# Two of eight dense chunks moved inside the last attention group of a transformer block, with the weight split spread over earlier groups

## The reference, cut to what matters

```
x = x + layernorm(attention(layernorm(x)))          # 4 x 1024 tokens, width 128
x = x + layernorm(ffn(layernorm(x)))

attention: 16 heads of width 8, q and k with rotary embedding and gelu, causal softmax, out projection
ffn(xf):   out = swiglu(xf, sWg, sWu, sWd)          # shared expert, 128 -> 256 -> 128
           for e in range(8):                       # top 2 of 8 experts by a softmax router
               out += w[:, e] * swiglu(xf, Wg[e], Wu[e], Wd[e])
swiglu(x, wg, wu, wd) = (silu(x @ wg) * (x @ wu)) @ wd
```

## Time and profile before

| | |
|---|---|
| median of three runs | 803.59 us (802.44 to 805.21) |
| the profiled execution: its time, its span | 806.09 us, 804.4 us |
| mean granted TensorE clock | 0.952 |
| busy in the span: PE, DVE, ACT, POOL | 667.4, 610.2, 505.1, 323.1 us |
| attention group 15 | 560.8 to 592.6 us |
| its end to the first tile pair | 592.6 to 622.2 us |
| tile pairs 0 to 35 with chunks 4 and 5 | 622.2 to about 768 us |

### The profile page before, as it was taken

How to read it: one execution, slowest core, us unless ns; L and a number is a source line. 1 busy time by engine, 2 the same in 40 slices (tenths; PEclk the granted TensorE clock), 3 DMA queues, 4 the chain that set the end, 5 groups by cost and what they waited for, 6 DMA issues and landing times.

```text
span 804.4 us, 17228 instructions
## 1 busy us (share of the span) xinstructions
PE 667.4 (83%) x6081; PEld 323.6 (40%) x6112; DVE 610.2 (76%) x1262; ACT 505.1 (63%) x1055; POOL 323.1 (40%) x437
## 2 busy tenths in 40 slices
PE   5786368999989889899879899888888889799961
PEld 2332022333334324234324334323246777587741
DVE  5989758888887897987897987987526476455667
ACT  3655036787767878687778677778656544344653
POOL 3675111122212233172533163533453137776642
PEclk9999569999999999999999999999799999899995
DMA  6446451120131131240230321202603112363534
GB/s 155 137 152 171 120 164 21 50 50 21 33 76 31 22 76 47 57 107 15 61 76 29 75 70 47 65 29 63 202 27 107 40 51 81 83 191 98 158 105 129
DMA packets 88785, 66.18 MB, mean 82 GB/s; under 512 B 27728, under 2 KB 75249, under 8 KB 88703
## 3 DMA queue, kind: packets, MB, share of 16 engines
q1 hardware_dynamic: 80076, 54.24, 26.5%
q0 software_dynamic: 4352, 8.99, 3.4%
q10 hardware_dynamic: 4274, 1.87, 0.9%
HBM read 38.11 MB, written 24.46 MB: 78 GB/s over the span
## 4 chain that ended last, share of the span: by engine, by line
PE 45%; DVE 22%; ACT 7%; issue 6%; POOL 3%; DMA 3%; SPq 2%; POOLq 0%; ACTq 0%; DVEq 0%
DVE block_max L343 13%; PE ps L1998 11%; PE ps L2025 8%; PE ps L328 5%; PE ps L2105 3%; ACT expT L1453 3%; PE ps L335 3%; PE ps L1975 2%; SPq L1194 2%; PE ps L2086 2%; PE ps L2094 1%; PE ps L2063 1%; DMA q_space<-negT 1%; PE ps L2088 1%; PE ps L2087 1%
## 5 line engine op out<-in xcount | busy, mean ns | idle before, releaser
L1453 ACT ACTIVATE expT<-ps 128x512 f32<-128x512 f32 (+1 forms) x640 | 325.3, 556 | 134.8 <-PE ps L2025 129.7
L343 DVE TENSOR_REDUCE block_max<-ps 128x8 f32<-128x1024 f32 x288 | 340.0, 1218 | 57.6 <-PE ps L328 38.7
L1998 PE MATMUL ps<-expT,vr 128*9 128x256 f32 (+1 forms) x2560 | 181.8, 366 | 16.5 <-ACT x_in L1413 14.9
L2025 PE MATMUL ps<-q_space,k_space 64*128 64x512 bf16 (+3 forms) x768 | 165.8, 338 | 10.0 <-DMA q_space<-negT 6.6
L1370 POOL TENSOR_SCALAR_AFFINE_SELECT expT<-expT 128x512 f32<-128x512 f32 x128 | 83.0, 661 | 195.5 <-ACT expT L1453 195.4
L328 PE MATMUL ps<-k_space,q_space 64*128 64x128 bf16 (+3 forms) x1152 | 132.0, 280 | 34.7 <-DVE block_max L343 24.4
L2025 PEld LDWEIGHTS ps<-q_space,k_space 64*128 64x128 bf16 x768 | 46.0, 94 | 153.2 <-ACT expT L1453 102.4
L1385 POOL DMA_INDIRECT expert_rows<-expT,tile_to x72 | 70.0, 973 | 59.1 <-ACT expT L1488 40.4
L1998 PEld LDWEIGHTS ps<-expT,vr 128*9 128x9 f32 x2560 | 42.1, 89 | 98.9 <-issue 47.1
L328 PEld LDWEIGHTS ps<-k_space,q_space 64*128 64x128 bf16 x1152 | 49.5, 95 | 74.0 <-DVE block_max L343 58.3
L1323 POOL TENSOR_SCALAR negs<-block_max 128x32 bf16<-128x32 f32 x16 | 4.7, 296 | 133.1 <-DVE block_max L1575 133.1
(11 more groups left out here) (235 smaller groups left out, 927.4 us busy)
## 6 DMA issues: line engine op xcount, KB each, us to landing
expT<-sorted_rows SPq DMA_DIRECT2D x72, 65.0 KB, 1.9
expT<-expert_rows SPq DMA_DIRECT2D x14, 256.0 KB, 5.1
q_parts<-parts SPq DMA_DIRECT2D x24, 128.0 KB, 2.3
k_parts<-parts SPq DMA_DIRECT2D x24, 128.0 KB, 2.3
q_space<-q_parts SPq DMA_DIRECT2D x32, 96.0 KB
k_space<-k_parts SPq DMA_DIRECT2D x32, 96.0 KB
v_ones<-v_st SPq DMA_DIRECT2D x8, 288.0 KB, 3.0
vr<-v_ones SPq DMA_DIRECT2D x16, 144.0 KB
```

Of the source, the lines that this page charges most:

```text
L343: nc.vector.reduce_max(bm[:, g % 2, 2 * f:2 * f + 2, at:at + 4], ps[:, 2 * odd:2 * odd + 2].rearrange("p h (n k) -> p h n k", k=P), AX_X). ...
L1453: act.activation(expT[:, (NS * g + s) % PTN, hh, 0:width], ps[:, B_S + n % S_RING, 0:width], ACT.Exp, scale=SCALE).then_inc(exp_ok, 1)
L1998: last = nc.tensor.matmul(ps[32 * hh:32 * hh + VW, B_O, at:at + n], vr[:, g % RING, kt, hh * VW:(hh + 1) * VW], expT[:, (NS * g + s) % PTN ...
L2025: last = nc.tensor.matmul(ps[:, B_S + n % S_RING, col:col + m], head_rows(kr, g, hh, slice(kt * P, (kt + 1) * P)), head_rows(qr, g, hh, sl ...
```

## The change

The shared expert on chunks 0 and 1 is computed inside group 15, on all engines:

- TensorE gets six new entries in its list (`AHEAD`): the gate passes of a half stand at its slot and the up passes at the slot behind, and the 16 down matmuls of a chunk take two slots. The list of units after the group starts at unit 4 (`FIRST_U`), and `chain` is shifted with it.
- silu is computed as x * (1 + tanh(x / 2)) / 2: ScalarE takes the tanh, VectorE multiplies in two instructions, and keeps the down result (ScalarE did that).
- `rows_ahead` on VectorE makes high and low parts of these two chunks at the end of group 14. SyncE fetches the chunks' rows in group 14.
- `w_hi` is made by ScalarE and `w_lo` by GpSimd, one expert at a time (128x512), in groups 1, 2, 3, 8 and 12. The down weights are loaded in group 13, and the padding of the spare region in group 1, where before all this stood in SyncE's queue during group 15.
- The last pair's scatters start behind tile pair 7, five at a time (before: behind 4, three at a time). Pads are written behind the load of pair 15 (before 12). The bank for one projection changes, and a wait moves from the first row transposes to the first transposes of h.

```diff
+AHEAD_C = 2
+FIRST_U = 2 * AHEAD_C
+AHEAD = {5: ("half", 0, 0), 8: ("half", 0, 1), 18: ("down", 0, 0), 20: ("half", 1, 0), 26: ("half", 1, 1), 33: ("down", 1, 0)}
+SPLIT = {1: (0, 1), 2: (2, 3), 3: (4, 5), 8: (6, 7), 12: (8,)}
...
+            if g == G - 1 and slot in AHEAD:
+                order.append((g, slot, *AHEAD[slot], None))
...
-            B_ROWS, B_PROJ = (B_Y, B_HT), (B_ONE, B_XT)
+            B_ROWS, B_PROJ = (B_Y, B_HT), (B_ONE, B_HT)
...
+                    if (g, slot) == (1, 24):
+                        sp.wait_ge(empty_ok, 2)
+                        sp.dma_start(xs_d[SPARE:].rearrange("(n p) w -> p n w", p=P),
+                                     empty[:].unsqueeze(1).to_broadcast([P, NE, XW])).then_inc(padded, DMA)
+                    if g == G - 3 and slot in (8, 26):
+                        rows = slice(P * (slot > 8), P * (slot > 8) + P)
+                        sp.wait_ge(lo_ok, NE + 1)
+                        sp.dma_start(w_gu[:, 0:NE, rows], wd_d[:, rows, :].rearrange("e k h -> k e h")).then_inc(down_in, DMA)
...
+                    if g == G - 2 and slot in (12, 16, 20, 24):
+                        sp.wait_ge(pv_done, NS * (G - 2))
+                        get_turned((slot - 12) // 4)
...
-                PADS_AT, HALF = 13, LATE_T // 2
+                PADS_AT, HALF = 16, LATE_T // 2
...
+                def low_weights(e):
+                    pool.wait_ge(hi_ok, e + 1)
+                    nc.gpsimd.tensor_tensor(w_lo[:, e], w_gu[:, e], w_hi[:, e], ALU.subtract).then_inc(lo_ok, 1)
...
+                    for at, e in zip((4, 6), SPLIT.get(g, ())):
+                        if s == at:
+                            low_weights(e)
...
-                first, each_time = 4, 3
+                first, each_time = 7, 5
...
+                def high_weights(e):
+                    if e == 0:
+                        act.wait_ge(late_in, DMA * LATE)
+                    act.activation(w_hi[:, e], w_gu[:, e], ACT.Copy).then_inc(hi_ok, 1)
+
+                def tanh(p, c, i):
+                    act.wait_ge(sh_gate, 2 * c + i + 1)
+                    wait(act, sh_hu, 2 * (c - 1) + i + 1)
+                    act.activation(tanhs[:, i], ps[:, bank_of(p)], ACT.Tanh, scale=0.5).then_inc(sh_silu, 1)
...
+                    for at, e in zip((8, 18), SPLIT.get(g, ())):
+                        if slot == at:
+                            high_weights(e)
...
-                    chain(u)
+                    chain(u - FIRST_U)
...
+                def rows_ahead(c):
+                    dve.wait_ge(xf_back[0], DMA * 2)
+                    v.tensor_copy(x_hi[:, c % 2], xf_in[:, c]).then_inc(x_hi_ok, 1)
+                    x_low(c)
+
+                def gated_ahead(p, c, i):
+                    dve.wait_ge(sh_up, 2 * c + i + 1)
+                    dve.wait_ge(sh_silu, 2 * c + i + 1)
+                    v.scalar_tensor_tensor(tanhs[:, i], tanhs[:, i], 1.0, ps[:, bank_of(p)], ALU.add, ALU.mult).then_inc(sh_mid, 1)
+                    dve.wait_ge(sh_mid, 2 * c + i + 1)
+                    wait(dve, sh_down, c)
+                    v.scalar_tensor_tensor(hu[:, i], tanhs[:, i], 0.5, ps[:, bank_of(p) + 1], ALU.mult, ALU.mult).then_inc(sh_hu, 1)
...
-                    if g == G - 1:
-
-                        dve.wait_ge(late_in, DMA * LATE)
-                        for i, es in enumerate((slice(0, 5), slice(5, NE + 1))):
-                            v.tensor_copy(w_hi[:, es], w_gu[:, es]).then_inc(hi_ok, 1)
-                            dve.wait_ge(hi_ok, i + 1)
-                            v.tensor_tensor(w_lo[:, es], w_gu[:, es], w_hi[:, es], ALU.subtract).then_inc(lo_ok, 1)
...
+                def up_ahead(p, c, i):
+                    three_passes(ps[:, bank_of(p) + 1], slice(INTER + P * i, INTER + P * (i + 1)), c).then_inc(sh_up, 1)
...
-                for u, (kind, n, i) in enumerate(UNITS):
+                for u, (kind, n, i) in list(enumerate(UNITS))[FIRST_U:]:
```

More of the change, by code:

```diff
@@ L1094, in block_kernel @@
             sh_silu = sem(two, "sh_silu")
+            sh_mid = sem(two, "sh_mid")
             sh_hu = sem(two, "sh_hu")
@@ L1235, in _ @@
                 load_chunk(sp, Z)
-                sp.wait_ge(lo_ok, 2)
-                for i in range(2):
-                    rows = slice(P * i, P * (i + 1))
-                    sp.dma_start(w_gu[:, 0:NE, rows], wd_d[:, rows, :].rearrange("e k h -> k e h")).then_inc(down_in, DMA)
-                    sp.dma_start(w_gu[:, NE, rows], swd_d[rows, :]).then_inc(down_in, DMA)
                 def get_mid(c):
@@ L1442, in side @@
                         exps(act, q)
+                    if g == G - 1:
+                        for p, _, at, kind, c, i, _ in of_group(g):
+                            if kind == "half" and slot == at + 1:
+                                tanh(p, c, i)
                     if (g, slot) == (G - 1, 36):
-                        x_high(0)
+                        x_high(AHEAD_C)
                 for g in range(G):
@@ L1681, in side @@
                         row_var_of(dve, q)
+                    if g == G - 2 and slot in (36, 38):
+                        rows_ahead((slot - 36) // 2)
+                    if g == G - 1:
+                        for p, _, there, kind, c, i, _ in of_group(g):
+                            if kind == "half" and slot == there + 2:
+                                gated_ahead(p, c, i)
+                            if kind == "down" and slot == there + 3:
+                                keep_ahead(p, c)
                     routes = (5, 6, 8, 10) if q == LAST - 1 else (15, 17, 20, 22)
@@ L1932, in reuse @@
                         pe.wait_ge(base_ok, 2)
+                    elif kind == "half":
+                        pe.wait_ge(sh_hu, 2 * g + WIDE[p - 2][4] + 1)
+                    elif kind == "down":
+                        pe.wait_ge(sh_kept, g + 1)
                     elif kind == "count":
@@ L1954, in item @@
                         ranks(pe, g, bank_of(p))
+                    elif kind == "half":
+                        pe.wait_ge(x_lo_ok, g + 1)
+                        pe.wait_ge(lo_ok, NE + 1)
+                        three_passes(ps[:, bank_of(p)], slice(P * which, P * (which + 1)), g).then_inc(sh_gate, 1)
+                    elif kind == "down":
+                        down_ahead(p, g, 0)
                     elif kind == "base":
@@ L2031, in _ @@
                                     item(p, *rest)
+                                if at == GH * s + hh - 1 and rest[0] == "half":
+                                    up_ahead(p, rest[1], rest[2])
+                                if at == GH * s + hh - 1 and rest[0] == "down":
+                                    down_ahead(p, rest[1], 1)
                             if hh % 2:
@@ L2161, in _ @@
                         tile_down(u - 1, before[1])
-                    elif u > 0 and before[2] == 1:
+                    elif u > FIRST_U and before[2] == 1:
                         shared_down(u - 1, before[1])
```

71 lines of the change are left out of this document (42 added, 29 removed).

## The result

| | before | changed |
|---|---|---|
| median of 12 executions each | 803.67 us (802.44 to 807.61) | 810.50 us (807.41 to 815.52) |
| ratio, 95% interval | | 1.0083 [1.0064, 1.0101] |
| profiled execution: its time, its span | 806.09, 804.4 us | 812.88, 811.2 us |
| mean granted clock | 0.952 | 0.951 |

The change makes the kernel 0.8% slower. The forecast was 804.0 us, no change; the time lies in its range (795 to 811), half a microsecond from the upper end, but the likeliest case was wrong by 6.4 us. The two profiled spans differ by 6.8 us as the medians do, so the traces can be set side by side. I cut them at starts that both have: the first of the two `negs<-left` on GpSimd, which end the row maxima of a group, for group 0 and for group 15 (computed late in the group before), the first half unit, and tile pairs 0, 8, 20 and 35.

A forecast was written before the change was run, and what follows sets the result against it. TensorE bounds, except VectorE's router chain early in group 15 and GpSimd's indirect DMA queue in the tile stage. Terms +1.0 + 6.0 - 6.6 = +0.4 us on the profiled 806.09, so 804.0 us against the median; range 795 to 811.

The forecast's parts named there:

- the new wait: Before the first tile pair: TensorE waits 4.8 us for the first row tiles, whose load waits for GpSimd's scatters.
- the ranks' wait: In group 15: TensorE waits 1.5 us or more for VectorE's router chain, which ends 2.95 us later.
- Split of the weights: Groups 1, 2, 3, 8, 12: ScalarE's copies cost 1.0 us; GpSimd's subtractions and VectorE's freed time count 0.
- Group 15: Group 15 grows 6 us: 2.95 up to the ranks, 6.5 of TensorE work behind, a shorter clock dip of about 5.
- First unit to first tile pair: Behind group 15: first tile pair starts 19.7 us after the first unit instead of 29.6, including a 4.8 us wait.
- To pair 8: Tile stage, first tile pair to pair 8: twelve units take 46.1 us instead of 43.7, so pair 8 starts at +65.8.
- To pair 20: Tile stage: GpSimd's queue makes TensorE wait 5.5 us for pair 19, until +104.9; with the clock, -6.6 us by pair 18.
- Behind pair 20: Rest of the kernel, 97 us: same units in the same order, so 0 change.
- The half clock case: Rival, 0.21: added matmuls in group 15 run at half clock, 808.1 us; 811 with another dip before the first tile pair.
- The full price of the split: Rival, 0.07: ScalarE's copies in the five groups cost 5.4 us instead of 1.0, giving 808.4 us.
- The tanh: Rival, 0.02: tanh in group 15 needs another ScalarE table, eight loads, 10.2 us, giving 814 us.

The follow-up runs named there:

- split alone: Kernel before with only the weights' parts made by ScalarE and GpSimd in groups 1, 2, 3, 8 and 12, not by VectorE: 806.3 us, ratio 1.0031.
- ahead_late: Changed kernel with the added halves and downs of chunks 0 and 1 moved behind the ranks (slots 14 to 34): 822.0 us, ratio 1.0228 to before.

## Where the forecast was right and wrong, step by step

The time is in the range by luck in part. The upper end, 811, belonged to a rival with two dips of the clock, one in group 15 and one behind the new wait; only the second came, and two other terms, the split and the end of the tile stage, made up the rest. The signs that the prediction named came: group 15 is 6.9 us longer (38.7 and 31.8), with a dip of 6.8 us instead of 13.6, TensorE waits 4.14 us for the first row tiles and 4.27 for pair 19. Only the ranks' wait is shorter than forecast, and the groups with two copies grew by 0.5 us instead of 0.2.

*Split of the weights (+1.0; measured +2.0 in the groups, 1.9 to 2.5 in the time).* The place was right (a copy at slot 18 ahead of the copy for which TensorE waits), the size was not: I gave four exposed copies 0.25 us each, where the row of 14.9 us in 25 waits said that TensorE was already waiting there and that each would be paid nearly in full, 0.51 of its 0.62 us. GpSimd's nine took 1.27 us each instead of 1.156 and held up nothing, as forecast. VectorE's freed time was worth nothing that shows, as forecast: stretch B is as long with the four instructions back as without. The split alone has a B shorter by 2.4 us, of which 3.4 us less at half clock can make up to 1.7.

*Group 15 (+6; measured +6.3, in the other traces with added work at slots 5 and 8 +4.4 to +6.8).* Right in sum, with errors that partly cancel. From the group's start to the ranks it is 15.2 us where it was 10.9 (+4.3, forecast +2.95), because VectorE waited 1.32 us for the up passes, a term that the sum lacked; the clock had fallen at 567.3 us, ahead of the first half at 569.03. The ranks' wait was 0.99 us, not 1.5. Behind the ranks it is +2.5 (forecast +2.9, with a dip of 5 us), and there was no dip. The last third of group 14, counted in B, is 0.5 us shorter. By the Trainium skill (TensorE: Matmul & The Clock Gate, Part 1, What's actually happening) activity releases the throttle; the traces agree in tendency only: by the granted clock, stretch B had 17.0 us at half before and 13.6 in the split alone, 3.4 to 10.2 us in the seven traces of this table with added work at slots 5 and 8, but 24 us in ahead_late, with the same work later. A short dip costs little there: 46.6 to 47.3 us with 3.4 us at half clock, 48.5 with 6.8, 49.0 with 10.2. So even with the clock up, group 15 keeps at least 4.4 of the 9.4 us of TensorE work that the units lose, and 6.8 against the split alone (39.8 us).

*First unit to first tile pair (19.7; measured 21.8).* The wait was forecast within 0.7 us. The step that failed is the sentence's end: down at 1.75 us. I took the new wait without the half clock behind it, although the longest wait in the trace of before (4.95 us, for the transposes at 700.90) was followed by 6.8 us of it, and had it only in a rival. Shorter waits don't settle it: the ranks' 1.50 us was followed by a dip, waits of 1.59 us at 596.85 and of 1.96 at 640.10 were not. In the ten traces of the first ten rows of the table every wait of TensorE of over 4 us in group 15 or the tile stage, twelve in all, has 3.4 to 10.2 us at half clock at its end or behind it. The same wait without the scatters' delay: 15.6, where I had written 15.

*To pair 8 (46.1; measured 46.2)*, right. *To pair 20:* the scatters of the last pair start 75.4 us behind the first unit (forecast 73.3, late by the 2.1 above), 20 operations later at 1.27 us the store goes out, and TensorE goes on at +105.6 (forecast 104.9). The landing and load took 4.9 us where I allowed 6. On this a page helps afterwards: the Trainium skill (DMA: Bandwidth & Descriptors, Anatomy of one DMA) gives 2.0 us and the bytes at 436 GB/s, by which I estimate 2.15 us for 64 KB. This store landed in 2.23 us; the one of before took 4.20, which the page's sum does not give.

*Behind pair 20 (0; measured +3.1, +1.2 or more in all eight traces of the table with the change).* This term was put at 0 because the units and their order are the same; the waits in it were not thought of. The first gather for the final sum takes 4.4 to 5.2 us in the kernels with the change and 3.4 and 2.8 in the two without (before, split alone), and VectorE and TensorE wait for it. Why the same transfer of 256 KB takes longer isn't known; no run tells it apart. Where the half clock follows the wait it adds about 2 us more (53.0 to 53.3 against 51.1 to 51.4).

*The rivals.* The half clock case had the two dips and 808 to 811 us; one of its dips came (behind the new wait), the other, behind the ranks, didn't. The full price of the split had the right mechanism at too high a price. The tanh cost no table load: ScalarE has none in group 15.

## What to carry to other kernels

Before work is moved forward, ask what the work behind it was hiding: here four halves covered the time in which GpSimd issued its last scatters, and without them TensorE waited 4.1 us and ran 6.8 us at half clock, together 6.2 us (21.8 against 15.6). A copy placed ahead of one that the bounding engine already waits for is paid nearly in full (0.51 of 0.62 us). A queue of equal operations can be counted before it is run, here within 2 us: moving them among each other chose which load was late, and at three at a time made the kernel 0.65% slower.

## What was not expected of the hardware

The kernel before took 803.7, 804.4 and 802.7 us in three measurements and 847.8 in a fourth, on another chip, with a spread of 0.6 to 1.7%. On that chip TensorE stood still for 5.7 and 8.7 us in one trace, and ScalarE and VectorE beside it. Their waits there have no releaser in the profile but "remote", as VectorE's in the same trace:

```profile
716.33 0.69 DVE L1785 COPY k_space<-ps 128x512 f32<-128x512 f32 x1 [9.36 <-remote]
```

No trace from the other chips has such a wait of over 2 us. In the four traces from that chip each one has indirect DMAs of GpSimd issued inside it, seven in this one, and the stretches that grew are those in which GpSimd issues many back to back (groups 8, 9, 12 and 13, pairs 8 to 20, and group 15 where the scatters were moved there). Groups 1 to 7, 10, 11 and 14 are within 0.4 us of the lengths on the first chip, leaving out the 0.5 us of the copies. So the time that this chip lost stands where indirect DMAs are issued; why it did so, and the others not, is open.

Even on the quiet chips the clock falls to half for 3 to 14 us somewhere in the groups of most executions (8 of 10), once behind a wait of TensorE of only 1.11 us (458.3 us in the changed kernel), which moves stretch A of the same kernel by up to 5 us (453.8 and 458.7). The dips of these eight start in one of three places, at 113 to 114, 330 to 335 or 456 to 467 us, and an execution has one to three of them. One profile of each side doesn't settle a difference of 1 or 2 us.
